# Attention with negated row maxima spread by a transpose of one repeated column, and totals of one block per head

## What is computed

```python
Q = (query @ Wq.T + bq)       # 16 heads of 32 channels
K = (key_value @ Wk.T + bk)
V = (key_value @ Wv.T + bv)
scores = einsum('bhqd,bhkd->bhqk', Q, K) / sqrt(32)
weights = softmax(scores, axis=-1)
attn = einsum('bhqk,bhkd->bhqd', weights, V)
x = x + attn @ Wo.T + bo
```

## Time and profile before

| | before |
|---|---|
| median of 3 runs | 2059.17 us (2056.53 to 2063.49) |
| the profiled execution | 2061.6 us, span 2059.8 us |
| mean granted TensorE clock | 0.983 |
| busy, PE / DVE / ACT / POOL | 1955.6 / 1422.5 / 929.9 / 1208.6 us |
| PE matmul instructions | 15620 |

### The profile page before, as it was taken

One profiled execution on the slowest core, in us unless ns is written; L12 is line 12 of the kernel. 1 busy time (PEld: TensorE's weight loads), 2 busy tenths in 40 slices (PEclk: granted clock), 3 DMA queues, 4 the chain that ended last, 5 costly groups with the idle time before them and its releaser, 6 DMA issues. The chain is left out here.

```text
span 2059.8 us, 41932 instructions
## 1 busy us (share of the span) xinstructions
PE 1955.6 (95%) x15620; PEld 1425.1 (69%) x15620; DVE 1422.5 (69%) x1479; ACT 929.9 (45%) x1332; POOL 1208.6 (59%) x862
## 2 busy tenths in 40 slices
PE   6989999999999999999998879989999999999998
PEld 5867777777777777777775557755555655758886
DVE  4126766676666666766766753489999999538775
ACT  4124444444444444444444544276677664533330
POOL 4126666666666666666656740069998997424210
PEclk9999999999999999999998889999999999999999
DMA  5545565555555555555544311040031002111201
GB/s 188 161 133 175 156 181 161 174 163 176 166 164 175 162 177 155 180 153 176 160 145 144 101 52 39 3 123 1 1 89 35 1 1 73 48 61 62 76 27 41
DMA packets 180570, 229.58 MB, mean 111 GB/s; under 512 B 21488, under 2 KB 111920, under 8 KB 174224
## 3 DMA queue, kind: packets, MB, share of 16 engines
q1 hardware_dynamic: 180368, 226.82, 35.7%
HBM read 153.18 MB, written 73.56 MB: 110 GB/s over the span
## 5 line engine op out<-in xcount | busy, mean ns | idle before, releaser
L504 POOL TENSOR_TENSOR a_half<-a_pt 128x1024 f32<-128x1024 f32 x128 | 307.1, 2399 | 345.8 <-ACT a_pt L571 336.3
L571 ACT ACTIVATE a_pt<-a_shift 128x2048 f32<-128x2048 f32 x128 | 245.1, 1915 | 475.4 <-PE a_o L887 371.7
L685 DVE TENSOR_TENSOR a_shift<-a_s,a_neg_rows 128x2048 f32<-128x2048 f32 x113 | 259.0, 2292 | 170.2 <-ACT a_neg_rows L588 170.2
L672 DVE TENSOR_REDUCE a_top<-a_s 128x128 f32<-128x2048 f32 x113 | 258.7, 2290 | 47.3 <-PE a_s L840 47.3
L1274 POOL TENSOR_TENSOR s_even_drive<-s_du,l_rows 128x512 f32<-128x512 f32 x128 | 162.9, 1273 | 61.6 <-DMA s_c_row<-bc_scratch 59.9
L799 PE MATMUL a_pj<-l_x_hi,l_w_hi 128*128 128x512 f32 x448 | 198.3, 443 | 0.0
L495 POOL TENSOR_TENSOR l_x_lo<-a_raw,l_x_hi 128x512 fp32r<-128x512 f32 x120 | 153.1, 1276 | 72.5 <-ACT l_x_hi L558 72.5
L799 PE MATMUL a_pj<-l_w_hi,l_x_hi 128*128 128x512 f32 x448 | 185.2, 413 | 0.0
L1282 POOL TENSOR_TENSOR s_odd_seen<-s_odd_state,s_c_row 128x512 f32<-128x512 f32 x128 | 162.5, 1270 | 34.9 <-DVE s_odd_state L1413 15.1
L1474 PEld LDWEIGHTS s_ps<-s_diag,s_du_t 128*128 128x128 f32 x1024 | 135.8, 194 | 62.0 <-issue 62.0
L801 PE MATMUL a_pj<-l_x_lo,l_w_hi 128*128 128x512 f32 x448 | 176.9, 395 | 0.1
(11 more groups left out here) (270 smaller groups left out, 4066.7 us busy)
## 6 DMA issues: line engine op xcount, KB each, us to landing
kv_scratch<-a_k_new SPq DMA_DIRECT2D x128, 256.0 KB, 2.5
kv_scratch<-a_v_new SPq DMA_DIRECT2D x128, 256.0 KB, 3.6
a_stack<-kv_scratch SPq DMA_DIRECT2D x512, 64.0 KB, 2.3
a_v<-kv_scratch SPq DMA_DIRECT2D x32, 1024.0 KB, 6.0
a_raw<-in_ctx SPq DMA_DIRECT2D x120, 256.0 KB, 3.3
a_q_stack<-q_scratch SPq DMA_DIRECT2D x128, 64.0 KB, 2.0
s_c_row<-bc_scratch SPq DMA_DIRECT2D x32, 256.0 KB, 5.7
e_ew_raw<-in_ew SPq DMA_DIRECT2D x8, 1024.0 KB, 4.8
```

The lines of the kernel that those rows point to most:

```text
L504: nc.gpsimd.tensor_tensor(half[:], w[:, 0:2], w[:, 2:4], ALU.add).then_inc(halved, 1)
L571: nc.scalar.activation(pt_head(g, p), shift[:].rearrange("p (i n) -> p i n", n=BANK), ACT.Exp).then_inc(exped, 1)
L672: dve.tensor_reduce(top[:], s_ps[:].rearrange("p i n -> p (i n)").rearrange("p (k q) -> p q k", q=L), AX.X, ALU.max).then_inc(blocked, 1)
L685: dve.tensor_tensor(shift[:].rearrange("p (k q) -> p k q", q=L), s_ps[:].rearrange("p i n -> p (i n)").rearrange("p (k q) -> p k q", q=L), ...
```

## The change

`neg_wide` and `widen_negative` are gone. PE turns `neg_max` itself, read as a 128 x 128 operand whose 128 columns are the same one; this stands one k earlier in PE's slot, ahead of the last three key matmuls. On ScalarE the copy now comes directly behind the exponentials, ahead of `split_head`. GpSimd adds a fourth step and leaves one block per head, `part` is half as large, and the totals are four calls, each with start and stop. In batch 7 the same spreading takes the place of `turn_last_negative`. In `mixer_in` GpSimd's memset first waits until the last attention output is stored, and ScalarE's wait for the padding moves to the first tile that needs it.

```diff
-        neg_wide = st.sb("neg_wide", [P, L])
-        part = st.sb("part", [P, 2, HG, 2 * L])
+        part = st.sb("part", [P, 2, HG, L])
...
-                nc.gpsimd.tensor_tensor(part[:, g % 2, p], fourth[:, 0:2 * L], fourth[:, 2 * L:], ALU.add).then_inc(parted, 1)
+                nc.gpsimd.tensor_tensor(fourth[:, 0:2 * L], fourth[:, 0:2 * L], fourth[:, 2 * L:], ALU.add).then_inc(paired, 1)
+                pool.wait_ge(paired, n + 1)
+                nc.gpsimd.tensor_tensor(part[:, g % 2, p], fourth[:, 0:L], fourth[:, L:2 * L], ALU.add).then_inc(parted, 1)
...
-            def widen_negative(n, fresh=False):
-                act.wait_ge(negated, n + 1)
-                if not fresh:
-                    act.wait_ge(neg_turned, n)
-                nc.scalar.activation(neg_wide[:], ones[:], ACT.Copy, scale=neg_max[:, 0:1]).then_inc(widened, 1)
...
                         exponentials(b, g, p, fresh)
+                        copy_negative(H * b + HG * g + p + 1)
                         if projects and not (final and g == CH - 1):
                             split_head(b + 1, g + 1, p)
-                        widen_negative(H * b + HG * g + p + 1)
-                        copy_negative(H * b + HG * g + p + 1)
...
-                    dve.wait_ge(widened, n)
+                    dve.wait_ge(spread, n)
...
-            def turn_negative(n, fresh=False):
-                pe.wait_ge(widened, n + 1)
-                if not fresh:
-                    pe.wait_ge(rows_out, n)
-                pe.transpose(m_ps[:, L:2 * L], neg_wide[:], ident[:]).then_inc(neg_turned, 1)
+            def spread_negative(n, at, fresh=False):
+
+                pe.wait_ge(negated, n + 1)
+                if not fresh:
+                    pe.wait_ge(rows_out, n)
+                pe.transpose(m_ps[:, at * L:(at + 1) * L], neg_max[:].to_broadcast([P, L]), ident[:]).then_inc(spread, 1)
...
-                    for j in range(2):
-                        for q in range(HG):
-                            mm = pe.matmul(o_ps[DH * q:DH * q + DH, L:2 * L], ones[:, :DH], part[:, g % 2, q, j * L:(j + 1) * L],
-                                           start=(j == 0), stop=(j == 1), tile_position=(0, DH * q))
+                    for q in range(HG):
+                        mm = pe.matmul(o_ps[DH * q:DH * q + DH, L:2 * L], ones[:, :DH], part[:, g % 2, q],
+                                       start=True, stop=True, tile_position=(0, DH * q))
...
                 turn_top(n)
-                keys(b + 1, g, p, p_ps[:, 0], range(2, KC))
-                turn_negative(n)
+                keys(b + 1, g, p, p_ps[:, 0], range(2, KC - 1))
+                spread_negative(n, 1)
+                keys(b + 1, g, p, p_ps[:, 0], range(KC - 1, KC))
...
-                turn_last_negative(h)
+                spread_negative(LAST + h, 2)
...
+            pool.wait_ge(ln.a_stored, 16 * KC * B)
             nc.gpsimd.memset(xc[:, :, :, 0:TW - 1], 0.0).then_inc(padded, 1)
...
-            act.wait_ge(padded, 1)
             take_projected(0)
...
             for n in range(KC, len(tiles)):
+                if n == G * KC:
+                    act.wait_ge(padded, 1)
```

More of the change, by code:

```diff
@@ L324, in attention @@
         p_ps = st.ps("pj", [P, 2, BANK])
-        (small_in, chi_out, clo_out, projected, k_out, v_out, ones_out, scored, blocked, top_turned, negated, widened,
-         neg_turned, rows_out, shifted, exped, halved, quartered, parted, weighed, totaled, inv_out, out_ready) = st.sems(
+        (small_in, chi_out, clo_out, projected, k_out, v_out, ones_out, scored, blocked, top_turned, negated,
+         spread, rows_out, shifted, exped, halved, quartered, paired, parted, weighed, totaled, inv_out, out_ready) = st.sems(
             "small_in", "chi_out", "clo_out", "projected", "k_out", "v_out", "ones_out", "scored", "blocked",
-            "top_turned", "negated", "widened", "neg_turned", "rows_out", "shifted", "exped", "halved", "quartered",
-            "parted", "weighed", "totaled", "inv_out", "out_ready")
+            "top_turned", "negated", "spread", "rows_out", "shifted", "exped", "halved", "quartered",
+            "paired", "parted", "weighed", "totaled", "inv_out", "out_ready")
         raw_in = st.sems(*[f"raw_in{k}" for k in range(KC)])
@@ L571, in exponentials @@
                 nc.scalar.activation(pt_head(g, p), shift[:].rearrange("p (i n) -> p i n", n=BANK), ACT.Exp).then_inc(exped, 1)
-            def widen_negative(n, fresh=False):
-                act.wait_ge(negated, n + 1)
-                if not fresh:
-                    act.wait_ge(neg_turned, n)
-                nc.scalar.activation(neg_wide[:], ones[:], ACT.Copy, scale=neg_max[:, 0:1]).then_inc(widened, 1)
             def copy_last_negative(h):
-                act.wait_ge(neg_turned, LAST + h + 1)
+                act.wait_ge(spread, LAST + h + 1)
                 act.wait_ge(shifted, half_no(h - 1, 1))
@@ L584, in copy_negative @@
             def copy_negative(n, fresh=False):
-                act.wait_ge(neg_turned, n + 1)
+                act.wait_ge(spread, n + 1)
                 if not fresh:
@@ L596, in _ @@
             act.wait_ge(ones_out, 1)
-            widen_negative(0, True)
             copy_negative(0, True)
@@ L651, in _ @@
                 if h + 1 < H:
-                    widen_negative(LAST + h + 1)
                     copy_last_negative(h + 1)
@@ L696, in negative_of_halves @@
                 dve.wait_ge(top_turned, half_no(h, 1))
-                dve.wait_ge(widened, LAST + h)
+                dve.wait_ge(spread, LAST + h)
                 dve.tensor_reduce(neg_max[:], m_ps[:, :2 * L], AX.X, ALU.max, negate=True).then_inc(negated, 1)
@@ L859, in turn_half @@
                 pe.transpose(m_ps[:, s * L:(s + 1) * L], (top_late if s else top)[:], ident[:]).then_inc(top_turned, 1)
-            def turn_last_negative(h):
-                pe.wait_ge(widened, LAST + h + 1)
-                pe.wait_ge(rows_out, LAST + h)
-                pe.transpose(m_ps[:, 2 * L:3 * L], neg_wide[:], ident[:]).then_inc(neg_turned, 1)
+            def spread_negative(n, at, fresh=False):
[3 more added lines that the diff above has]
+                pe.transpose(m_ps[:, at * L:(at + 1) * L], neg_max[:].to_broadcast([P, L]), ident[:]).then_inc(spread, 1)
             def turn_top(n, fresh=False):
@@ L904, in _ @@
             turn_top(0, True)
-            turn_negative(0, True)
+            spread_negative(0, 1, True)
             def weigh_last(b, g, p, first):
```

## The result

The changed kernel took 2044.61 us (median of 4 executions, 2042.34 to 2051.23) beside 2058.88 for the kernel before: ratio 0.9934, 95% interval 0.9912 to 0.9956, a gain of 14.3 us where 21.2 were forecast. The profiled execution is the slowest of the four, with a span of 2049.4 us (2059.8 before).

The account below looks back on a forecast made before the run. TensorE was taken as nearly full in the main loop, a chain between engines as the bound in batch 7. Gains 14.1 + 0.9 + 5.3 + 0.9 = 21.2 us from 2059.17 gave 2038 us; range 2025 to 2051.

Parts of the forecast that it names:

- Part 1: Main-loop slots: spreading moves to TensorE, three matmuls forward; shift ends 0.69 us earlier, its wait at the slot's end goes.
- rival 1: Time handed back: tile change costs 0.31, p=2 keeps 0.16, 128-column add takes 0.73; gain 8 us, 2051; chance 0.17.
- allowance of 0.03 per slot: Every main-loop slot: 0.03 us added because the repeated column's load can no longer be made ahead.
- Part 2: Totals in slot p=3: four matmul calls instead of eight, saving 0.23 us of TensorE.
- Part 3: Slot p=0, end of group on DVE: the weights' wait for `out_ready` goes, slot 8.60 becomes 8.09 us.
- Part 4: GpSimd's extra add costs 0.45 us per head and delays the split: new 0.27 us TensorE wait at p=0.
- The sum per group: Four main-loop slots: 8.09, 8.09, 8.29, 8.36 make 32.83 us, 32.95 with the allowance, against 33.51.
- The loop edges: Two slots around each of six loop edges: 17.73 us spares 0.40; with the other two slots 0.47 each, 2.8 us.
- The last main slot and batch 7: Last main-loop slot gains 0.9 us; batch 7 gains 0.44 at 12 of 15 spreading waits, 5.3, plus 0.9 from totals.
- Rival 3: Batch 7's granted clock changes: less waiting raises it, 2028 us (chance 0.06), or the shorter chain loses more, 2048 (0.04).
- 1 and 2: The second: TensorE waits at the transpose's new place, 0.39 us in 112 slots, 44 us; 2086 us, chance 0.07.

Follow-up runs that it names:

- the run with the old place: Changed kernel with the spreading transpose put back behind all key matmuls, repeated column kept: 2054.73 us, ratio 0.9979.
- the run with the part undone: Changed kernel with GpSimd's last addition and the totals as in the kernel before (16 total matmuls a group, not 8): 2036.20 us, ratio 0.9882.
- the parts undone: Changed kernel with GpSimd's one 128x256 addition, two-block parts and the old totals restored: 2036.20 us, ratio 0.9882.
- the changed kernel again: The changed kernel measured once more, nothing altered, to see whether its loop edges repeat: 2047.09 us, ratio 0.9937.
- the split first with 48 instructions: Changed kernel with GpSimd's split ahead of its two narrow additions and 48 wait instructions added on TensorE ahead of the loop: 2025.93 us, ratio 0.9838.
- the two runs that differ in the query loads alone: Changed kernel with GpSimd's split ahead of its narrow additions and 48 added waits: 2025.93 us; the same with next-batch query loads issued earlier: 2038.02 us.
- the queries early: Changed kernel with the next batch's four query loads issued at the end of slot p=2 instead of at p=3: 2042.32 us, ratio 0.9912.

## Why the prediction was right, and where it was not

- **Part 1: right, with a slip and a wrong reason.** Place, load and hand-overs came within 0.01 us. The shift ends 0.74 ahead of the load, not 0.6; but the 0.6 was a slip, since the prediction's own times give 0.73 (715.45 to 715.89, and 0.29). It said that TensorE starts its next tile 0.31 us behind its last matmul "because of the shift"; with the shift out of the way that step takes 0.32 (rival 1's figure, where 0.29 was chosen), so the shift ended about when TensorE was ready anyway, and what its place cost in a group, 0.46 us by the run with the old place, stood at p=2 and p=0 but for 0.05. The 0.03 too little did not show in the sum, because the last values matmul stands up to 0.04 us earlier in its slot than the 7.80 forecast (7.76 at p=1, 7.79 at p=2). The allowance of 0.03 per slot for the load was not needed. p=1 and p=2 came to 8.09, as forecast; the 0.16 us at p=2 went, and the run with the old place brought it back.
- **Part 2: right.** Loads of the totals 0.24 us (forecast 0.23), slot p=3 8.26 (8.29).
- **Part 3: right.** The wait for `out_ready` is gone: at p=0 DVE's product ended at 713.12, 0.55 ahead of the weights at 713.67, where before they loaded 0.12 behind it.
- **Part 4: right.** Add 0.46 us (0.45), wait 0.27 us at 21 places (0.27), slot p=0 8.37 (8.36). That this wait cancels part 2 stood in the numbers and not in the text; the run with the part undone shows it.
- **The sum per group: right.** 32.81 us against 32.83 without, 32.95 with the allowance.
- **The loop edges: wrong.** The prediction took 17.73 us for the pair of slots and subtracted 0.40, as if the rest of it were a fixed price, and that six times; only five edges have a jump (the pair at the first pass took 17.01 us before). It had the edge as a place where "TensorE is kept back anyway" and never asked by what. The price hangs on where the body starts and ends in the stream of instructions, and the change moved both; it also hangs on what is in the DMA queues at the jump. Forecast 17.33 us, measured 19.73; with 48 instructions that give the start its old place back and keep the end clear of a multiple, 17.39, and with the parts undone, 17.42. Five edges at 2.4 us are 12 us, in the profiled run more than the whole shortfall (forecast 21.2, there 2059.8 - 2049.4 = 10.4).
- **The last main slot and batch 7: right, but one pair of traces could not have told.** 0.9 as forecast; batch 7 gained 5.4 us of 6.2, and the waits for the spreading shrank by 0.43 us each (0.44), at all 15 heads and not at 12. But that stretch scatters: by the same marks it took 128.1 to 137.9 us, mean 132.0, in the ten traces here that have the changed kernel's code in batch 7, and 137.1, 138.0 and 140.9, mean 138.7, in the three with the old code. The windows of the changed kernel again and of the split first with 48 instructions are

```profile
1082.12:1214.17 132.05, 103.32 (x1261) 66.01 (x1257) 98.52 (x134) 65.47 (x73) 96.34 (x80) 0.88 0.33 102
```
```profile
1063.38:1191.50 128.12, 100.58 (x1261) 64.91 (x1257) 98.58 (x134) 65.45 (x73) 96.42 (x81) 0.91 0.34 105
```

  The granted clock goes 0.85, 0.88, 0.91 as the length goes 135.5, 132.1, 128.1. Rival 3's link of clock and length is there, without any change of the code; which of the two drives the other is not shown.
- **Rivals.** 1 and 2 did not come, though rival 1's change of tile did. No rival had the edge in it, though it took 12 us.
- **The number.** 2044.61 us lies between the stated 2025 and 2051 by luck as much as by merit: the room above 2038 was there for rivals 1 and 3, and the loss at the edges, which the prediction had not priced, happened to fit into it.

With the place put right, the change is worth 2035.45 against 2059.51 us, 24 us where 21.2 were forecast.

The Trainium skill (Runtime: NRT & Kernel Launch, Instruction fetch mechanics) does say that instructions come in blocks of 16 KiB fetched ahead in sequence, and that a taken branch whose target lies outside the current window stalls until it is fetched. The traces agree, with one or two packets at a jump of 3.4 to 6.3 us; that the place of the body's end within a block decides between one and two, and the place of its start over a second stop, is from the runs here alone. By it the 17.73 us of the earlier trace rows was an open term and not a constant.

## What to carry to other kernels

Adding or removing instructions inside a hardware loop also moves its ends in the instruction stream; where the engine of the loop is full, compare the slots at the edges by themselves, and count the instruction packets there, before judging the change in the body. If they got worse, a few waits in an idle place ahead of the loop can put them back: here 48 instructions of them were worth 10 us, two thirds of the change itself, while 112 cost 8 us, so the number has to be worked out from both ends of the body. And of several waits that a change adds, ask whether the order on the slower engine can be turned: moving the split ahead of two additions cost nothing and gave back all of it.

## What the runs showed of the hardware beyond that

- A body that begins late in a packet stops a second time, when the rest of that packet is used up: 1.2 to 1.9 us with 124 instructions left, 2.9 to 3.5 us with 44, nothing visible with 188 or more. Why the stop with 44 left came ahead of the first matmul and not in the midst of the scores is open.
- An instruction packet can come later or sooner with the data transfers issued around it. It started 0.2 to 3.3 us behind the jump, and the two runs that differ in the query loads alone show that they move it. What exactly it waits for is open: the late ones (1.8 us or more) stood 2.7 to 3.7 us behind the issue of a value store, but at the third edge with the queries early the packet came 1.4 us behind that store, in the same order of issues.
- A 128x128 transpose whose stationary operand is one column read 128 times loads in 0.13 us, no slower than 128 different columns (0.14).
- Waits that are already fulfilled are not free: 256 instructions of them (512 waits), all ahead of the first matmul, moved it by 26.3 us (9.08 to 35.40), about 0.1 us an instruction.
